# First experts' results combined inside the second self-attention, with a new order of its products

## The chip, the cores and the metric

The kernel runs on one core of a Trainium2 chip. The metric is the device time of one launch in microseconds. The engines are named PE or TensorE (matmul; PEld is its weight load), DVE or VectorE, ACT or ScalarE, POOL or GpSimd, and SP, which issues transfers.

## The reference

A decoder of two layers on 16 sequences (batches) of 256 tokens with 256 features, all float32. The part that the change touches:

```
# layer 0: the last step, a mixture of experts (8 experts, 2 for each token)
n  = layernorm(x)                      # (x - mean) / sqrt(var + 1e-5)
o  = w0(token) * E_i(n) + w1(token) * E_j(n)      # E(n) = gelu(n Wup) Wdown, the token's two best experts
x  = x + (n + layernorm(o))
# layer 1: self-attention, 16 heads of 64
n  = layernorm(x)
q, k, v = n Wq + bq, n Wk + bk, n Wv + bv
x  = x + softmax(q k^T / 8) v Wo + bo  # softmax over the keys, head by head
```

After it come layer 1's cross-attention and its mixture of 64 experts. Matmuls whose inputs are called high and low are float32 products split in three (high high, high low, low high).

## The kernel before, in words

x stays in SBUF as 32 tiles of 128 tokens (`sh.x`), two to a batch; `sh.stats` holds mean and variance of each token, `sh.rstd` the inverse root. The kernel is a row of blocks; within a block each engine runs its own program in order, and semaphores order them; a block ends for all engines together. `clear_semaphores` is a block of its own that resets the counters used so far.

The stretch around the change:

- `l0_experts_tiles` ends with the experts' rows written to a table in DRAM (`scratch.results`).
- `l0_experts_combine` (L3033) is a block for all 32 tiles in groups of four. POOL gathers two rows for each token (L3066); ACT scales the first (L3078); DVE adds the second, scaled (L3104), and takes the statistics of the sum (L3108, L3111); ACT takes the square root (L3084), DVE its reciprocal and an offset (L3117 to L3119); ACT scales x and adds the offset (L3091); DVE adds the normalised sum (L3126) and takes the statistics of the new x (L3131, L3134). In the same block the weights of the coming attention are loaded by SP (L1368), split into high (ACT, L1377) and low (DVE, L1382), and the bias of v is multiplied by Wo on TensorE (L1396).
- `clear_semaphores`, then `norm_scales` (L284), a block that makes `sh.rstd` of all 32 tiles with ACT's square root and DVE's reciprocal.
- `l1_attention` (L1406) goes over the batches, from -1 to 16. A batch has eight slots h, one for each pair of heads. In a slot TensorE makes the scores of pair h (L1499), turns the probabilities of pair h-3 (L1508), makes products called pieces, and multiplies the probabilities of pair h-4 with v (L1519). DVE takes the maximum of the scores (L1648), inverts the sums of pair h-1 (L1653), copies the turned probabilities (L1660), takes the low part of the output of pair h-5 (L1664) and the low parts of the pieces (L1670, L1674). ACT makes the exponents (L1574) and the high parts (L1598, L1584, L1587) or the copy of v (L1592). POOL multiplies the probabilities by the inverted sums (L1623) and adds the output bias to x once a batch (L1634).
- The pieces are in `order` (L1450): C is the key and query product of a pair, V a quarter of v, W half of the output product (L1684 adds it to x, and after the second half L1688 takes the new statistics), X the turning of half of the normalised x (L1531). Each names its number, how many batches it is ahead, and its slot. Pieces go to two PSUM banks in turn (`fill[i % 2]`), and a piece waits until the one before it in its bank is drained. The high and low parts of the output, `outT`, have one buffer for a batch; ACT therefore waits for W of the batch before, before it takes out the first pair (L1597).
- Scores have one PSUM buffer, so the scores of a pair wait for the exponents of the pair before it (L1494). The normalised x of the next batch (L1642) is made at the end of slot 2.
- The loop over the batches is rolled for batches 3 to 14 on every engine.

Of the kernel before, what the change touches and what calls it, by code (L numbers as in the profile page):

```python
# [14 lines left out]
P = 128  # L15
# [250 lines left out]


ROOT_GUESS = float(0x5f3759df)
ROOT_STEPS = 14


def inverse_root(engine, step, out, var, spare):


    step.then(engine.tensor_scalar(var, var, EPS, None, ALU.add))
    step.then(engine.tensor_scalar(out.bitcast(I32), var.bitcast(I32), -0.5, ROOT_GUESS, ALU.mult, ALU.add))
    for n in range(3):
        step.then(engine.tensor_tensor(spare, out, out, ALU.mult))
        step.then(engine.tensor_tensor(spare, spare, var, ALU.mult))
        step.then(engine.tensor_scalar(spare, spare, -0.5, 1.5, ALU.mult, ALU.add))  # L280
        step.then(engine.tensor_tensor(out, out, spare, ALU.mult))
# [1124 lines left out]
def l1_attention(nc, sh, prepared):  # L1406
# [11 lines left out]
    with ExitStack() as ctx:  # L1418
# [17 lines left out]
        outT = both("outT", [P, PAIRS, SEQ])  # L1436
        parts = sb("parts", [P, TPB, 6])
        means = sb("means", [P, TPB, 2])
# [5 lines left out]
        per_batch = {"X": KC, "C": PAIRS, "V": 4, "W": TPB}  # L1444
# [8 lines left out]
        assert len(order) % 2 == 0 and len(order) == sum(per_batch.values())  # L1453
# [5 lines left out]
        def prior_in_bank(i, b):  # L1459


            back = 0
            while True:
                i -= 2
                if i < 0:
                    i, back = i + len(order), back + 1
                if isinstance(b, int) and b - back < -1:
                    return None
                kind, number, ahead = order[i][0:3]
                if live(b - back + ahead):  # L1470
                    return kind, done(kind, number, b - back + ahead)

        def over_batches(engine, batch):


            for b in range(-1, 3):
                batch(b)
            with engine.Fori(3, BATCH - 1) as b:
                batch(b)
            batch(BATCH - 1)  # L1480
            batch(BATCH)

        def lagging(b, h, lag):

            own, pair = (b, h - lag) if h >= lag else (b - 1, PAIRS + h - lag)
            return (own, pair) if live(own) else None

        with nc.Block() as block:

            @block.tensor  # L1490
            def _(pe):
# [31 lines left out]
                def piece(i, kind, number, own, b):  # L1523
                    bank = fill[i % 2]
# [3 lines left out]
                    if kind == "X":  # L1528
                        pe.wait_ge(s_xn, own + 1)
                        for t in range(TPB):  # L1530
                            last = pe.transpose(bank[:, t * P:(t + 1) * P], xn[:, t, number * P:(number + 1) * P], sh.ident[:])  # L1531
# [11 lines left out]
                    elif kind == "W":  # L1543
                        t = number
                        pe.wait_ge(s_olow, PAIRS * (own + 1))
                        last = split_product(pe, bank[:, 0:DIM], [([a[:, c, t * P:(t + 1) * P] for a in outT],
# [3 lines left out]
                def batch(b):  # L1550
                    for h in range(PAIRS):
# [7 lines left out]
                        for i, kind, number, ahead in pieces:  # L1559
                            piece(i, kind, number, b + ahead, b)  # L1560
# [6 lines left out]
            def _(act):  # L1567
# [10 lines left out]
                def drain(i, kind, number, own):  # L1578
                    bank = fill[i % 2]
# [3 lines left out]
                    if kind == "X":  # L1583
                        act.copy(xT[0][:, number, :], bank[:, 0:SEQ]).then_inc(high["X"], 1)  # L1584
# [9 lines left out]
                def take_out(b, h):  # L1594
# [3 lines left out]
                    act.copy(outT[0][:, h, :], o_ps[h % 2][:, 0:SEQ]).then_inc(s_ohigh, 1)  # L1598

                def batch(b):  # L1600
                    for h in range(PAIRS):
                        taking = lagging(b, h, TAKE)
                        last_pair = taking and taking[1] == PAIRS - 1
                        if last_pair:
                            take_out(*taking)
                        if live(b):
                            exponents(b, h)
                        if taking and not last_pair:
                            take_out(*taking)
# [1864 lines left out]
```

## Time and profile before

| | us |
|---|---|
| median of 3 runs | 3141.59 (3135.95 to 3143.5) |
| the profiled execution | 3120.02 |
| its span | 3118.3 |
| mean granted TensorE clock | 0.907 of full speed |

| engine | busy us | share of the span |
|---|---|---|
| PE | 2555.6 | 82% |
| PEld | 2131.8 | 68% |
| DVE | 2057.3 | 66% |
| ACT | 1424.4 | 46% |
| POOL | 881.3 | 28% |

The shares are means over stages that differ: the combine takes some 100 us, the attention after it some 830 us. A number in brackets behind a row of the timeline is the idle time of that engine just before the instruction, and behind the arrow stands what ended it.

### The profile page before, as it was taken

Reading aid. Unit: us, or ns where it says so; the run is one execution under the profiler, and the core shown is the slowest. Engines: PE = TensorE matmul, PEld = TensorE weight load, DVE = VectorE, ACT = ScalarE, POOL = GpSimd, SP = SyncE. Lnnn points to the kernel's source line nnn. Section 1 sums busy time; section 2 is a strip of 40 time slices with the busy share of each in tenths; the row PEclk is TensorE's granted clock in tenths of the full one; section 3 lists DMA queues with packets and bytes.
Section 4 is the critical chain, followed back from the end, with each engine's and each line's share of the span. In section 5 each row is a group of like instructions: output and inputs, shape, how many; then the busy total and the mean of one; then the engine's idle time right before and its main releaser. Section 6 shows DMA issues by size and latency. Waiting matters only on the chain. (4 is left out here: it accounts for less than half of the span.)

```text
span 3118.3 us, 59168 instructions
## 1 busy us (share of the span) xinstructions
PE 2555.6 (82%) x19764; PEld 2131.8 (68%) x19764; DVE 2057.3 (66%) x4353; ACT 1424.4 (46%) x3350; POOL 881.3 (28%) x1026
## 2 busy tenths in 40 slices
PE   5978699999862999999149999999999679997483
PEld 4866588888752999999137777777777666665131
DVE  5863698989643777776566666666666547775664
ACT  1520334343330777776345554555454337665032
POOL 0000345454316000000633333333333103333266
PEclk8987799999975999999569999999999889999576
DMA  8000000000077765654400000000000463221745
GB/s 286 0 2 0 1 1 0 0 0 0 27 259 265 270 227 210 228 210 151 146 26 1 1 0 0 0 0 0 0 0 1 142 190 89 83 84 30 241 132 169
DMA packets 165273, 270.61 MB, mean 87 GB/s; under 512 B 21088, under 2 KB 140592, under 8 KB 151856
## 3 DMA queue, kind: packets, MB, share of 16 engines
q1 hardware_dynamic: 151008, 226.14, 21.5%
q0 software_dynamic: 9216, 25.18, 2.5%
q10 hardware_dynamic: 4944, 17.96, 1.5%
q8 instruction: 57, 0.93, 0.1%
q14 instruction: 48, 0.39, 0.0%
HBM read 191.85 MB, written 77.37 MB: 86 GB/s over the span
## 5 line engine op out<-in xcount | busy, mean ns | idle before, releaser
L1623 POOL TENSOR_TENSOR a_prob<-a_prob,a_rden 128x1024 f32<-128x1024 f32 x128 | 242.6, 1895 | 574.1 <-DVE a_rden L1653 574.1
L1574 ACT ACTIVATE a_prob<-a_s_ps,a_ntop 128x256 f32<-128x256 f32 x512 | 236.0, 473 | 353.8 <-DVE a_ntop L1648 353.8
L3066 POOL DMA_INDIRECT e0c_ya<-sorted_results,e_slots x64 | 67.9, 1061 | 507.8 <-POOLq L2869 488.6
L2306 DVE TENSOR_REDUCE x1a_top<-x1a_s_ps 128x4 f32<-128x1024 f32 x128 | 155.9, 1222 | 82.0 <-PE x1a_s_ps L2134 80.7
L2231 ACT ACTIVATE x1a_prob<-x1a_st_ps,x1a_mask_now 128x512 f32<-128x512 f32 x256 | 162.3, 686 | 91.5 <-PE x1a_st_ps L2150 90.1
L1648 DVE TENSOR_REDUCE a_ntop<-a_s_ps 128x4 f32<-128x1024 f32 x128 | 156.3, 1221 | 67.0 <-PE a_s_ps L1499 67.0
L1161 ACT ACTIVATE x0b_sq<-x0b_f 128x1024 f32<-128x1024 f32 x64 | 67.9, 1060 | 282.4 <-DVE x0b_f L1235 282.3
L68 PE MATMUL e0x_up_ps<-e0x_xT_high,e0x_up_w_high 128*128 128x256 f32 x624 | 180.4, 289 | 1.7 <-DVE e0x_up_w_low L2997 1.7
L68 PE MATMUL e0x_up_ps<-e0x_xT_high,e0x_up_w_low 128*128 128x256 f32 x624 | 177.6, 285 | 0.0
L68 PE MATMUL e0x_up_ps<-e0x_xT_low,e0x_up_w_high 128*128 128x256 f32 x624 | 177.4, 284 | 0.0
L68 PE MATMUL e0x_y_ps<-e0x_down_w_high,e0x_hT_high 128*128 128x256 f32 x624 | 176.6, 283 | 0.0
L68 PE MATMUL e0x_y_ps<-e0x_down_w_low,e0x_hT_high 128*128 128x256 f32 x624 | 176.6, 283 | 0.0
L68 PE MATMUL e0x_y_ps<-e0x_down_w_high,e0x_hT_low 128*128 128x256 f32 x624 | 176.6, 283 | 0.0
L1660 DVE COPY a_pT<-a_pT_ps 128x512 f32<-128x512 f32 x256 | 161.0, 670 | 0.7 <-PE a_pT_ps L1508 0.7
L1664 DVE TENSOR_TENSOR a_outT_low<-a_o_ps,a_outT_high 128x256 fp32r<-128x256 f32 x128 | 54.1, 423 | 149.0 <-ACT a_outT_high L1598 149.0
L1519 PE MATMUL a_o_ps<-a_pT,a_v 128*64 128x256 f32 x1024 | 141.4, 398 | 1.2 <-DVE a_outT_low L1664 1.2
L1508 PE MATMUL a_pT_ps<-ident,a_prob 128*128 128x128 f32 x1024 | 141.2, 281 | 0.0
L1674 DVE SCALAR_TENSOR_TENSOR a_kqT_low<-a_fill,a1w_kq_bias,a_kqT_high 128x256 fp32r<-128x256 f32 x256 | 109.3, 478 | 44.8 <-ACT a_kqT_high L1587 44.8
L3011 DVE TENSOR_TENSOR e0x_hT_low<-e0x_h,e0x_hT_high 128x512 fp32r<-128x512 f32 x156 | 104.4, 689 | 37.8 <-ACT e0x_hT_high L2977 37.8
L1508 PEld LDWEIGHTS a_pT_ps<-ident,a_prob 128*128 128x128 f32 x1024 | 110.5, 141 | 18.3 <-issue 1.6
L68 PEld LDWEIGHTS e0x_up_ps<-e0x_xT_high,e0x_up_w_high 128*128 128x128 f32 x624 | 120.7, 193 | 2.1 <-issue 2.1
L68 PEld LDWEIGHTS e0x_up_ps<-e0x_xT_low,e0x_up_w_high 128*128 128x128 f32 x624 | 120.6, 193 | 0.0
(579 smaller groups left out, 8520.2 us busy)
## 6 DMA issues: line engine op xcount, KB each, us to landing
e0x_up_raw<-up_rows SPq DMA_DIRECT2D x39, 1024.0 KB, 4.9
e0x_down_raw<-down_rows SPq DMA_DIRECT2D x39, 1024.0 KB, 5.6
x_qk<-head_rows SPq DMA_DIRECT2D x384, 64.0 KB
head_rows<-x1p_rows_out SPq DMA_DIRECT2D x32, 512.0 KB, 3.7
e1w_ew<-in_L_ffn_expert_w_dram SPq DMA_DIRECT2D x8, 2048.0 KB, 18.1
sorted_tokens<-zeros SPq DMA_DIRECT2D x10, 1024.0 KB, 12.4
e0x_xg<-sorted_tokens SPq DMA_DIRECT2D x39, 256.0 KB, 2.8
sorted_results<-e0x_y SPq DMA_DIRECT2D x39, 256.0 KB, 2.2
```

The lines of the kernel that those rows point to most:

```text
L68: last = pe.matmul(out, a[x], b[y], start=at == 0, stop=at == n - 1)
L1161: act.activation(sq[:, side % 2, :], f[:, p, side, :], ACT.Square).then_inc(s_sq, 1)
L1508: last = pe.transpose(pT_ps[n][:, j, t * P:(t + 1) * P], prob[:, h % RING, n, t, j * P:(j + 1) * P], sh.ident[:])
L1519: last = pe.matmul(o_ps[h % 2][DH * n:DH * (n + 1), 0:SEQ], v[:, j, at:at + DH], pT[:, h % 2, n, j, :], start=j == 0, stop=j == TPB - 1)
L1574: last = act.activation(prob[:, h % RING, n, t, :], s_ps[:, n, t * SEQ:(t + 1) * SEQ], ACT.Exp, bias=ntop[:, h % RING, n, t:t + 1], accum_ ...
L1623: last = pool.tensor_tensor(p, p, scale_of, ALU.mult)
L1648: dve.tensor_reduce(ntop[:, h % RING], s_ps[:].rearrange("p n (t s) -> p n t s", t=TPB), AXIS.X, ALU.max, negate=True).then_inc(s_top, 1)
L1660: dve.tensor_copy(pT[:, h % 2, n], pT_ps[n][:]).then_inc(s_pT, 1)
L1674: last = dve.scalar_tensor_tensor(kqT[1][:, number, side, :], bank[:, side * SEQ:(side + 1) * SEQ], kq_bias[:, side, number:number + 1], k ...
L2231: last = act.activation(prob[:, c % 2, j, 2 * (h % 2):2 * (h % 2) + 2, :], st_ps[:, :, j * SEQ:(j + 1) * SEQ], ACT.Exp, bias=mask_now[:, p ...
L2306: dve.tensor_reduce(dst, s_ps[h % 2][:].rearrange("p n (t s) -> p n t s", t=TPB), AXIS.X, ALU.max).then_inc(s_max, 1)
L3011: dve.tensor_tensor(part[1], h[:, n, :], part[0], ALU.subtract).then_inc(s_hl, 1)
```

## The change

- `clear_semaphores` goes ahead of the combine block; the one behind it and the `norm_scales` of the attention go.
- `l0_experts_combine` now combines batch 0 alone, beside the same loading and splitting of the weights. It gathers the rows of batches 0 and 1.
- The steps of the combine are methods of a class `Combine`, for one batch each. In batch b of the attention the combine of batch b+2 goes on: DVE mixes in slot 0, takes the statistics in slot 1; POOL makes the inverse root in slot 2; DVE makes the offset in slot 3; ACT scales x at the end of slot 3; DVE adds in slot 4 and takes the statistics of x in slot 5; POOL makes the second inverse root in slot 6. POOL gathers the rows of batch b+3 in slots 3 to 6, and ACT scales the first rows of batch b+3 at the end of slot 7. The normalisation of batch b+1 in slot 2 waits for its second root.
- The inverse roots are made by `inverse_root`, three Newton steps from an integer guess, 14 dependent small operations, and no longer by ACT's square root.
- `order` names the bank of each piece as its last number; x is turned in one piece of four transposes instead of two; the output product moves from slots 4 and 5 to 5 and 6; `outT` has two buffers.
- The rolled loop now holds two batches in each turn (batches 3 to 12) and POOL's program is not rolled.

```diff
-        order = [("C", 2, 0, 0), ("V", 0, 0, 0), ("C", 3, 0, 1), ("V", 1, 0, 1), ("C", 4, 0, 2), ("C", 5, 0, 3),
-                 ("C", 6, 0, 3), ("W", 0, -1, 4), ("C", 7, 0, 5), ("W", 1, -1, 5), ("V", 2, 0, 6), ("V", 3, 0, 6),
-                 ("X", 0, 1, 6), ("X", 1, 1, 6), ("C", 0, 1, 7), ("C", 1, 1, 7)]
+        order = [("C", 2, 0, 0, 0), ("V", 0, 0, 0, 1), ("C", 3, 0, 1, 0), ("V", 1, 0, 1, 1), ("C", 4, 0, 2, 0), ("C", 5, 0, 2, 1),
+                 ("C", 6, 0, 3, 0), ("C", 7, 0, 3, 1), ("V", 2, 0, 4, 0), ("V", 3, 0, 4, 1), ("W", 0, -1, 5, 0), ("X", 0, 1, 6, 0),
+                 ("W", 1, -1, 6, 1), ("C", 0, 1, 7, 0), ("C", 1, 1, 7, 1)]
...
-        outT = both("outT", [P, PAIRS, SEQ])
+        outT = both("outT", [P, 2, PAIRS, SEQ])
...
-                        wait_past(act, filled["W"], TPB * b)
+                        wait_past(act, filled["W"], TPB * (b - 1))
...
 # ACT, at the end of a slot
+                        if h == PAIRS - 1 and live(b + 3):
+                            combine.first(act, b + 3)
+                        if h == 3 and live(b + 2):
+                            combine.scale_x(act, b + 2)
...
 # POOL, in a slot
+                        if h == 2 and live(b + 2):
+                            combine.mix_root(pool, b + 2)
+                        if 3 <= h <= 6 and live(b + 3):
+                            combine.gather(pool, b + 3, h - 3)
+                        if h == 6 and live(b + 2):
+                            combine.x_root(pool, b + 2)
...
 # DVE, between the copies of the turned probabilities and the low part of the output
+                        if live(b + 2):
+                            if h == 0:
+                                combine.mix_rows(dve, b + 2)
+                            if h == 1:
+                                combine.mix_stats(dve, b + 2)
+                            if h == 3:
+                                combine.offset(dve, b + 2)
+                            if h == 4:
+                                combine.add(dve, b + 2)
+                            if h == 5:
+                                combine.x_stats(dve, b + 2)
...
+    def mix_rows(self, dve, c):
+        step.counted(dve.tensor_scalar(self.grow[:], sh.rstd[:, tiles], 1.0, None, ALU.add))
+        step.counted(dve.tensor_tensor(self.less[:], sh.stats[:, tiles, 0], sh.rstd[:, tiles], ALU.mult))
+        for t in range(TPB):
+            dve.wait_ge(self.s_first, TPB * c + t + 1)
+            dve.scalar_tensor_tensor(self.out[:, t, :], self.ya[:, t, 1, :], self.weights[:, 1, bass.ds(TPB * c + t, 1)],
+                                     self.out[:, t, :], ALU.mult, ALU.add).then_inc(self.s_mix, 1)
+    def offset(self, dve, c):
+        dve.wait_ge(self.s_r2, c + 1)
+        step.then(dve.tensor_tensor(self.shift[:], self.stat[:, :, 0], self.r2[:], ALU.mult))
+        dve.scalar_tensor_tensor(self.shift[:], self.shift[:], -1.0, self.less[:], ALU.mult, ALU.subtract).then_inc(self.s_shift, 1)
...
 # the block ahead of the attention, ACT and DVE
+                following.high(act, 0)
+                following.high(act, 1)
+                combine.first(act, 0)
+                following.high(act, 2)
+                combine.scale_x(act, 0)
+                following.high(act, 3)
+                combine.first(act, 1)
...
+                following.low(dve, 0)
+                following.low(dve, 1)
+                combine.mix(dve, 0)
+                combine.mix_root(dve, 0)
+                combine.offset(dve, 0)
+                following.low(dve, 2)
+                following.widen(dve)
+                combine.add(dve, 0)
+                combine.x_stats(dve, 0)
+                combine.x_root(dve, 0)
+                following.low(dve, 3)
+                following.bias_taken(dve)
```

## Rows read from the trace of the kernel before

**Rows 1.** busy time of each engine in two stretches; columns: stretch, us, busy us (instructions), TensorE clock, DMA share, GB/s.
```profile
1488.00:1595.00 107.00, 5.95 (x16) 4.58 (x16) 72.25 (x242) 41.13 (x78) 67.90 (x64) 0.53 0.40 122
...
2002.00:2053.00 51.00, 47.59 (x400) 38.93 (x400) 33.09 (x69) 26.27 (x94) 16.40 (x9) 1.00 0.00 0
```

**Rows 2.** timeline at the ends of the combine; columns: start us, us, engine, line, operation, tiles.
```profile
1489.79 0.18 DVE L3097 TENSOR_SCALAR e0c_grow<-x_rstd 128x32 f32<-128x32 f32 x1 [2.63 <-PEq L2869]
...
1590.39 1.40 DVE L3131 BATCH_NORM_STATS2 e0c_parts<-x_resident 128x6 f32<-128x256 f32 x4
...
1591.83 0.38 DVE L3134 BATCH_NORM_AGGREGATE x_stats<-e0c_parts 128x2 f32<-128x6 f32 x4
...
1593.56 0.18 DVE L298 TENSOR_SCALAR n_var<-x_stats 128x32 f32<-128x32 f32 x1 [1.35 <-PEq L108]
...
1595.00 0.74 DVE L1642 TENSOR_SCALAR a_xn<-x_resident,x_stats,x_rstd 128x256 f32<-128x256 f32 x2 [0.54 <-PEq L293]
...
1597.92 0.55 PE L68 MATMUL a_fill<-a_xT_high,a1w_wk_high 128*128 128x256 f32 x1 [1.01 <-DVE a_xT_low L1670]
```

**Rows 3.** DMA issues of 1487 to 1596: KB each, us from issue to landing.
```profile
a1p_w_nat<-in_L_attn_Wk_dram SPq DMA_DIRECT2D x1, 1024.0 KB, 8.5
```

**Rows 4.** timeline inside the combine, ACT and DVE.
```profile
1500.02 0.51 ACT L3078 ACTIVATE e0c_out<-e0c_ya,e_weights 128x256 f32<-128x256 f32 x1 [1.40 <-DMA e0c_ya<-sorted_results,e_slots]
...
1531.08 0.18 DVE L3117 RECIPROCAL e0c_r<-e0c_std 128x4 f32<-128x4 f32 x1
...
1531.29 0.16 DVE L3118 TENSOR_TENSOR e0c_shift<-e0c_stat,e0c_r 128x4 f32<-128x4 f32 x1
```

**Rows 5.** instructions by line, 1487 to 1596: busy us, mean ns, idle before.
```profile
L3104 DVE SCALAR_TENSOR_TENSOR e0c_out<-e0c_ya,e_weights,e0c_out 128x256 f32<-128x256 f32 x32 | 14.4, 482 | 26.1 <-ACT e0c_out L3078 26.1
...
L1382 DVE SCALAR_TENSOR_TENSOR a1w_wq_low<-a1p_w_nat,a1w_wq_high 128x2048 fp32r<-128x2048 f32 x1 | 2.3, 2282 | 0.0
```

**Rows 6.** TensorE's waits in the attention, 1600 to 2410: us in total, times, longest.
```profile
PE a_fill L1531 <- ACT a_v L1592: 29.0, 15, 2.1
...
PE a_fill L68 <- DVE a_outT_low L1664: 13.3, 15, 1.0
...
PE a_s_ps L1499 <- DVE a_kqT_low L1674: 5.3, 15, 0.4
```

**Rows 7.** timeline of DVE in one batch of the attention, 2002 to 2054.
```profile
2002.76 1.23 DVE L1648 TENSOR_REDUCE a_ntop<-a_s_ps 128x4 f32<-128x1024 f32 x1 [1.09 <-PE a_s_ps L1499]
...
2026.33 1.22 DVE L1648 TENSOR_REDUCE a_ntop<-a_s_ps 128x4 f32<-128x1024 f32 x1
...
2029.89 0.42 DVE L1664 TENSOR_TENSOR a_outT_low<-a_o_ps,a_outT_high 128x256 fp32r<-128x256 f32 x1 [1.09 <-ACT a_outT_high L1598]
...
2030.64 1.66 DVE L1674 SCALAR_TENSOR_TENSOR a_kqT_low<-a_fill,a1w_kq_bias,a_kqT_high 128x256 fp32r<-128x256 f32 x4 [0.32 <-ACT a_kqT_high L1587]
...
2032.54 1.21 DVE L1648 TENSOR_REDUCE a_ntop<-a_s_ps 128x4 f32<-128x1024 f32 x1
...
2053.72 1.23 DVE L1648 TENSOR_REDUCE a_ntop<-a_s_ps 128x4 f32<-128x1024 f32 x1 [1.09 <-PE a_s_ps L1499]
```

**Rows 8.** costliest groups of the page, the exponents.
```profile
L1574 ACT ACTIVATE a_prob<-a_s_ps,a_ntop 128x256 f32<-128x256 f32 x512 | 236.0, 473 | 353.8 <-DVE a_ntop L1648 353.8
```

**Rows 9.** timeline of POOL in the next stage, an inverse root.
```profile
2600.72 0.22 POOL L275 TENSOR_SCALAR x1a_gvar<-x1a_gvar 128x2 f32<-128x2 f32 x1
...
2604.95 1.24 POOL L2294 TENSOR_SCALAR x1a_gn<-x_resident,x_stats,x_rstd 128x256 f32<-128x256 f32 x1
```

**Rows 10.** timeline where POOL and DVE run together, and gathers.
```profile
699.71 1.90 POOL L1048 TENSOR_TENSOR x0b_f<-x0b_f,x0b_rnorm 128x1024 f32<-128x1024 f32 x1
...
699.77 2.92 DVE L1266 TENSOR_TENSOR x0b_g<-x0b_f,x0b_rnorm 128x1024 f32<-128x1024 f32 x1
...
1523.28 0.95 POOL L3066 DMA_INDIRECT e0c_ya<-sorted_results,e_slots  x1 [0.30 <-issue]
...
1525.78 2.64 POOL L3066 DMA_INDIRECT e0c_ya<-sorted_results,e_slots  x1 [0.31 <-issue]
```

More of the change, by code:

```diff
@@ L265 @@
 STATS_STEPS = 3
[L268 to L281, printed above, removed]
 def norm_scales(nc, sh, name, twice=False):
@@ L1476, in over_batches @@
             for b in range(-1, 3):
[L1477 to L1481, printed above, removed]
+                batch(b, b % 2)
+            with engine.Fori(1, (BATCH - 4) // 2) as pair:
+                for p in range(2):
+                    batch(2 * pair + (1 + p), 1 - p)
+            for b in range(BATCH - 3, BATCH + 1):
+                batch(b, b % 2)
         def lagging(b, h, lag):
@@ L1529, in piece @@
                         pe.wait_ge(s_xn, own + 1)
-                        for t in range(TPB):
-                            last = pe.transpose(bank[:, t * P:(t + 1) * P], xn[:, t, number * P:(number + 1) * P], sh.ident[:])
+                        for k in range(KC):
+                            for t in range(TPB):
+                                last = pe.transpose(bank[:, k * SEQ + t * P:k * SEQ + (t + 1) * P], xn[:, t, k * P:(k + 1) * P],
+                                                    sh.ident[:])
                     elif kind == "C":
@@ L1583, in drain @@
                     if kind == "X":
-                        act.copy(xT[0][:, number, :], bank[:, 0:SEQ]).then_inc(high["X"], 1)
+                        act.copy(xT[0][:].rearrange("p k s -> p (k s)"), bank[:]).then_inc(high["X"], 1)
                     elif kind == "C":
@@ L3030, in _ @@
                 over_groups(dve, step)
[L3033 to L3053 removed]
+ROOT_GUESS = float(0x5f3759df)
@@ new lines, in inverse_root @@
+def inverse_root(engine, step, out, var, spare):
+    step.then(engine.tensor_scalar(var, var, EPS, None, ALU.add))
+    step.then(engine.tensor_scalar(out.bitcast(I32), var.bitcast(I32), -0.5, ROOT_GUESS, ALU.mult, ALU.add))
+    for n in range(3):
+        step.then(engine.tensor_tensor(spare, out, out, ALU.mult))
+        step.then(engine.tensor_tensor(spare, spare, var, ALU.mult))
+        step.then(engine.tensor_scalar(spare, spare, -0.5, 1.5, ALU.mult, ALU.add))
+        step.then(engine.tensor_tensor(out, out, spare, ALU.mult))
@@ L3094, in _ @@
+                following.high(act, 1)
[4 more added lines that the diff above has]
+                combine.first(act, 1)
             @block.vector
             def _(dve):
-                step = Steps(dve, s_own)
-                dve.tensor_scalar(grow[:], sh.rstd[:], 1.0, None, ALU.add)
-                step.then(dve.tensor_tensor(less[:], sh.stats[:, :, 0], sh.rstd[:], ALU.mult))
@@ L3100, in mix @@
-                def mix(g):
-                    for t in range(g * G, (g + 1) * G):
-                        dve.wait_ge(s_first, t + 1)
-                        dve.scalar_tensor_tensor(out[:, g % OUTS, t % G, :], ya[:, t % GATHERS, 1, :], weights[:, 1, t:t + 1],
-                                                 out[:, g % OUTS, t % G, :], ALU.mult, ALU.add).then_inc(s_mix, 1)
-                    dve.wait_ge(s_mix, (g + 1) * G)
-                    for i in range(G):
-                        last = dve.bn_stats(parts[:, i, :], out[:, g % OUTS, i, :])
-                    step.then(last)
-                    for i in range(G):
-                        last = dve.bn_aggr(stat[:, g % 2, i, :], parts[:, i, :])
-                    step.then(last)
-                    dve.tensor_scalar(std[:, g % 2, :], stat[:, g % 2, :, 1], EPS, None, ALU.add).then_inc(s_var, 1)
```

239 lines of the change are left out of this document (132 added, 107 removed).

## The prediction

> **What bounds the kernel now.** I read the busy time by stretch first. The reader is to see two stretches in it [rows 1]: from 1488 to 1595 TensorE works 5.95 of 107 us and DVE, ACT and POOL share the work; in one batch in the middle of the attention (2002 to 2053) TensorE is busy 47.59 of 51 us at the full clock of 2.4 GHz, DVE 33.09, ACT 26.27, POOL 16.40. So the combine stage has no matmul that matters, and the attention is a TensorE stage whose other engines have room. Second, the timeline at the seams [rows 2]: the combine's DVE starts at 1489.79, its last statistics end at 1592.2, a block that clears semaphores and one for the square root follow, the attention starts at 1595.00 and the first key product at 1597.92. Third, TensorE's waits in the attention [rows 6]: 29.0 us before the transpose of x (15 waits, for the ACT copy of v), 13.3 us before the output product (15, for outT_low), 5.3 us before scores (15, for kqT_low). Fourth, the DVE rows of one batch [rows 7], which show how the slots of a batch (one for each pair of heads) are chained: maximum, exponents on ACT, drains, next maximum. The batch lasts 2053.72 - 2002.76 = 50.96 us.
>
> **1. The combine stage becomes the combine of batch 0 beside the weights.** Removed: 1595.00 - 1489.79 = 105.2 us [rows 2]. What stands in its place, on DVE, which is last in it:
> - The clearing block now stands ahead: 1593.56 - 1592.21 = 1.35 us, so the stage starts at 1491.15 [rows 2].
> - Wk lands 8.5 us after its issue [rows 3], which is in the stage's first half microsecond: 1500.1. Its high part on ACT takes as the others do about 1.9 us (1502.0), its low part on DVE 2.28 [rows 5]: 1504.3. Batch 0's rows are there by then: the second tile's ACT step began at 1500.02 [rows 4], 1501.4 with the clearing.
> - Mixing: two small operations and two of 0.48 [rows 5], 1.15 with their waits; statistics of two tiles 1.4 (four cost 1.40 + 0.38 [rows 2], and the two added settles and memsets take back what half the tiles save). 1506.9.
> - The root by Newton steps: 15 dependent small operations at 0.21 (1531.29 - 1531.08 [rows 4]): 3.1; offset 0.4: 1510.4.
> - Low part of Wv 2.28, widening of the bias about 1.8, add 0.95, statistics of x 1.4, second root 17 x 0.21 = 3.5, low part of Wo 2.28: 1522.7. The bias product (TensorE's 5.95 us of [rows 1]) lies under the last four. Taking it 0.4 and the block's end 0.5: **1523.7**.
> This saves 1595.0 - 1523.7 = **71.3 us**. Ends: small operations at POOL's 0.28 instead of 0.21 (+2.2) and weights 5 us later give 64; DVE never waiting for Wk gives 75.
>
> **2. The batch before the first pays for batch 1.** Its DVE order is now mix, statistics, wait for POOL's root, offset, wait for ACT's scaling, add, statistics, and only then the low part of xT, for which all key products wait. From the attention's start: normalise 0.74, mix 1.15, statistics 1.4, POOL's root 15 x 0.28 = 4.2 (2600.72 to 2604.95 for the same steps [rows 9]), offset 0.4, ACT 1.15, add 0.95, statistics 1.4, low part of xT 0.7: first key product after some 12.5 instead of 1597.92 - 1595.00 = 2.9 us. **+9.6 us**. Here nothing covers it. In batch 0 no pairs wait to be turned and there is no output product, so its first slots are set by the chain of maximum, exponents and drains and not by TensorE; some of the combine's DVE work and ACT's first scaling show: **+1.5**, between 0 and 5.
>
> **3. The new order of products.** TensorE's work in a batch stays: 50.96 less its waits of 2.09 + 0.94 + 0.37 = 47.6 us. With named banks x is turned into bank 0 after an output product that DVE drained a slot earlier, and no longer behind two v products, so the 29.0 us go. The output product moves from slot 4 to slot 5, one slot after outT_low of the last pair is made, so the 13.3 us go. **-42.3 us**. The second outT buffer removes an ACT wait (ACT held the first pair until the output product was through), which was covered; alone I cost it at nothing, but it lets the first product move later.
>
> **4. What the combine puts into each batch.** DVE: 1.15 (slot 0), 1.4 (1), 0.4 (3), 0.95 (4), 1.4 (5), together 5.3 us; ACT: four operations of 0.5, 2.1 us; POOL: two roots, 4.2 + 4.7, and four gathers of 0.95 + 0.30 [rows 10], 14 us. POOL then works 30 of 48 us. Its product of a pair (1.9 us) is wanted by TensorE two slots later, 11 us, so the 4.2 us of a root behind it are covered. DVE's steps stand between the pT copies and the low part of outT, where it now idles about a microsecond for ACT: in the slot that begins at 2026.33 the low part starts at 2029.89, +3.56, after 1.09 us of idle time, so the copies ended at +2.5 [rows 7]. So 1.0 us of each is free, and the rest has room in slots that TensorE sets (5.8 us against a chain of 5.2 in those with one key product). Where they hurt:
> - Slots 2 and 3 now both drain two key products. In slot 3 of before the drain ends 5.9 us after the maximum (2030.64 + 1.66 - 2026.33), the last pair's outT_low is squeezed in, and the next maximum comes at +6.21 [rows 7]. Slot 2 becomes such a slot and has xn (0.73) as well: 6.65; slot 3 gets ACT's scaling of x (1.1 us) ahead of the last pair's outT_high: 7.0. TensorE needs 5.8 in each, lets the maximum lag, and is held only where exponents end (3.3 us after the maximum began: 1.2 for itself, four of 0.47 [rows 8] and the handoffs) later than it arrives: my sum over the slots gives 0.55 us at the start of slot 5.
> - Slot 6 drains x and then the output product with statistics: the next maximum is 0.4 us later, and the 0.37 us wait for the first key product becomes 0.65.
> - Taken off: 0.25 us of transposes that wait in slot 4.
> That is 0.58 us a batch: **+8.7 us** for 15. The floor is 0 (TensorE set everything); the ceiling, if none of it were covered, is 5.3 + 2.1 = 7.4 us a batch, 111 us.
> POOL's root ends 8.75 us after slot 2's maximum, and DVE asks for it at 9.3: the offset does not wait, by half a microsecond.
>
> **A contention that the trace shows.** DVE's product with two inputs in SBUF took 2.92 us when it began inside POOL's multiplication, of which only 1.08 lie after that one's end (699.71 + 1.90); and a gather's issue took 2.64 us where DVE's low part of Wq, 2.28 us and also with two such inputs, ran, and 0.95 without [rows 5, 10]. The combine's mixing and adding (two SBUF inputs) begin 2.5 us after a maximum and POOL's product runs until about +3.25: 0.7 us of delay in slots 0 and 4, which have that room. The Trainium skill ("SBUF — State Buffer", Who interferes with whom) states that a DVE instruction with two SBUF inputs contends with a GpSimd instruction that reads SBUF, and that whoever starts second is fully blocked; on the first pair the trace agrees. The page infers that such a DVE instruction leaves descriptor generation alone; on the second the trace disagrees, and the measurement decides. By the page the gathers would cost nothing more, by the row up to 0.5 us each, in either case on POOL with 18 us to spare: the sum is the same unless this grows, which is rival A.
>
> **Sum**: -71.3 + 9.6 + 1.5 - 42.3 + 8.7 = **-93.8 us**. The profiled execution took 3120.0 us (span 3118.3), so its like would take 3026. The median of the runs shown is 3141.6, 0.7% above the profiled one; the time that I name goes by the median: 3141.6 - 94 = **3047.6 us**.
>
> **The rivals.**
> - A. The layout's gain is eaten: the drains of slots 2 and 3, the blocked DVE steps and the handoffs over POOL and ACT hold TensorE some 2.8 us a batch instead of 0.58 (the 42 us come back). For it: DVE goes from 33 to 38.5 us a batch, 79% of 48.5, with two slots over 6.6 us in a row. Against: they lag without holding TensorE in my sum. -60 us, 3082. Chance 0.2.
> - B. Everything is covered and the short stage is at its better end: -106, 3036. For it: slot 2 of before had 1.3 us of lag that TensorE never felt. Against: slot 3's ACT order is certain to be longer. 0.12.
> - C. The short stage is not short: the weights, their splits, roots and the bias product form one line on DVE and take 60 us instead of 32. Against: every term has a row. -66 and less, 3076. 0.05.
> - D. Slower. DVE's offset waits in slot 3 for POOL's root, with the drains of two key products and outT_low behind it, and TensorE behind them. The saving without this is 102.5 us; spread over 15 batches it is lost from 6.8 us of wait a batch, that is, from a root of 11.0 us instead of 4.2. For it: POOL's product, the bias addition and the root are one queue and the margin is only 0.5 us. Against: 0.28 us a step where POOL does it now [rows 9]. At 8 us a batch the time is +18, 3160. 0.04.
> - E. The forecast, within 3032 and 3066: 0.59.
> A change under 0.3%, 9 us, cannot be told from none. Cases E, B, A and C are faster: 0.95 with a little of D's approach to zero left to same (0.01); slower 0.04. The range takes in A and B and the bounds of points 1 and 4: 3025 to 3092.
>
> **What would show it.** Right: first attention instruction about 34 us after the combine block's first, first key product 12 us later; no wait of the x transpose for a_v, none of the output product for outT_low; a batch of 48.2 to 48.8 us between like maxima; POOL near 60% busy with POOL never named by TensorE. Wrong: waits of DVE's offset for r2, of ACT's first step for the gathers, or of scores for a_prob in every batch (A or D); a batch over 50 us (A); over 40 us between the first DVE instruction of the combine and the attention's start (C).

## The result and the profile after

| | median, us | runs | ratio to before, 95% |
|---|---|---|---|
| before | 3140.3 (3135.95 to 3143.5) | 4 | |
| after | 3017.03 (3011.59 to 3022.18) | 4 | 0.9608 [0.9586, 0.9630] |
| forecast | 3047.6 (range 3025 to 3092) | | 0.970 |

The change takes 123 us off, 29 more than forecast, and the time lies 8 us below the range. The profiled execution of after took 3018.96 us (span 3017.3), near its median; that of before had taken 3120.0, below its own. Stages that the change does not touch move between executions: the experts before the combine took 638.8 us in the profile of before and 649.1 in that of after, and the two profiled spans differ by 101.0 us only. So I compare stage by stage.

The page of after, its busy time by engine:

```profile
span 3017.3 us, 59401 instructions
PE 2543.4 (84%) x19764; PEld 2126.7 (70%) x19764; DVE 2098.6 (70%) x4492; ACT 1414.3 (47%) x3324; POOL 970.7 (32%) x1491
```

Busy time by stretch, the short stage and one batch, as in [rows 1] (stretch, us, then PE, PEld, DVE, ACT, POOL busy, clock, DMA share, GB/s):

```profile
1499.00:1534.00 35.00, 6.13 (x16) 4.69 (x16) 21.49 (x70) 10.33 (x10) 7.63 (x8) 0.60 0.51 162
1833.00:1880.00 47.00, 45.37 (x386) 37.53 (x386) 39.18 (x90) 27.66 (x97) 26.72 (x44) 1.00 0.04 13
```

The first row has what [rows 1] showed in 107 us; the second shows a batch in 47 us instead of 51, DVE 6 us and POOL 10 us busier in it. The timeline at the seams, as in [rows 2]: the experts' last copy, the low part of the weights that stands first in DVE's new stage, the attention's first instruction and the first key product:

```profile
1498.66 0.69 DVE L3036 COPY e0x_y<-e0x_y_ps 128x512 f32<-128x512 f32 x1 [5.06 <-PE e0x_y_ps L68]
...
1509.52 2.29 DVE L1366 SCALAR_TENSOR_TENSOR a1w_wq_low<-a1p_w_nat,a1w_wq_high 128x2048 fp32r<-128x2048 f32 x1 [10.17 <-ACT a1w_wq_high L1361]
...
1533.46 0.74 DVE L1646 TENSOR_SCALAR a_xn<-x_resident,x_stats,x_rstd 128x256 f32<-128x256 f32 x2 [0.54 <-PEq L3188]
...
1545.11 0.55 PE L68 MATMUL a_fill<-a_xT_high,a1w_wk_high 128*128 128x256 f32 x1 [9.74 <-DVE a_xT_low L1675]
```

From the experts' last copy to the attention's start it is 1533.46 - 1498.66 = 34.8 us; in before it was 1595.00 - 1486.47 = 108.5. The price is in the last row: the first key product starts 11.65 us into the attention and TensorE has waited 9.74 us for xT_low, where [rows 2] had 2.9 and 1.01. TensorE's waits in the attention (us in total, times, longest), as in [rows 6]:

```profile
PE a_s_ps L1490 <- DVE a_kqT_low L1679: 12.7, 15, 2.0
...
PE a_fill L68 <- DVE a_xT_low L1675: 9.7, 1, 9.7
PE a_s_ps L1490 <- ACT a_prob L1567: 8.4, 15, 1.4
```

The waits for v are gone, and those for outT_low ahead of the output product too but for one of 1.0 us; scores wait more, for kqT_low (5.3 us in [rows 6]) and for the exponents (5.1 in before).

Where the time went, from the profiles (attention: from its first DVE instruction to the first of the next norm, in before 1595.00 to 2429.32, in after 1533.46 to 2324.26):

| | forecast | measured |
|---|---|---|
| the stage between the experts and the attention | -71.3 | -73.7 |
| attention | -22.5 | 790.8 - 834.3 = -43.5 |
| all other stages | 0 | +16.2 |

### The profile page after: what moved, and what is told of

Its sections match the earlier page's. It is cut to its first block and busy times, and to the rows that moved or that the text cites. A ratio compares the mean times of both kernels' runs of the same rounds, so it can differ in the third digit from the quotient of the medians.

```text
span 3017.3 us, 59401 instructions
## 1 busy us (share of the span) xinstructions
PE 2543.4 (84%) x19764; PEld 2126.7 (70%) x19764; DVE 2098.6 (70%) x4492; ACT 1414.3 (47%) x3324; POOL 970.7 (32%) x1491
## 5 line engine op out<-in xcount | busy, mean ns | idle before, releaser
L1018 POOL TENSOR_TENSOR x0b_tree<-x0b_f 128x1024 f32<-128x1024 f32 x32 | 76.4, 2389 | 156.5 <-DVE x0b_f L1219 154.2
L2976 ACT CAST e0x_xT_high<-e0x_t_ps 128x512 fp32r<-128x512 f32 x39 | 22.9, 587 | 218.3 <-PE e0x_t_ps L2937 218.3
```

The lines of the kernel that those rows point to most:

```text
L1018: step.then(pool.tensor_tensor(tree[:], src[:, :, 0:HD // 2], src[:, :, HD // 2:HD], ALU.add))
```

## The experiments

### The layout alone, the combine alone, the second buffer alone

Three kernels that each do one part of the change. The layout alone takes over the order, the banks, the one piece in which x is turned and two output buffers, and leaves the combine its own stage. The combine alone keeps the order, the banks, x in two pieces and one output buffer (here and below the lines with a minus are those of the kernel after):

```diff
- order = [("C", 2, 0, 0, 0), ("V", 0, 0, 0, 1), ..., ("W", 0, -1, 5, 0), ("X", 0, 1, 6, 0), ("W", 1, -1, 6, 1), ...]
+ order = [("C", 2, 0, 0), ("V", 0, 0, 0), ..., ("W", 0, -1, 4), ("C", 7, 0, 5), ("W", 1, -1, 5), ("V", 2, 0, 6), ...]
- outT = both("outT", [P, 2, PAIRS, SEQ])
+ outT = both("outT", [P, 1, PAIRS, SEQ])
```

The third is the kernel before with `outT` of two sides, the take-out of pair 0 waiting for the output product of the batch before the last (`TPB * (b - 1)`). Because the side of the buffer goes by parity, its loop holds two batches in each turn, as in after, and POOL's program is not rolled; all three kernels have this in common.

> The new order of products with named banks and two output buffers, with the combine stage of before in front. Theory M (the gain of the layout was mis-sized: in the trace of after a steady batch has 46.6 us of TensorE work and 0.9 us of waits where before had 50.96 in all, so removing a wait also removes the slow restart around it): a batch of 46.9 to 47.2 us, the attention some 60 us shorter than before, the kernel 58 to 62 us faster (3078 to 3082). Rival F (the forecast's sizes, 42 us of removed waits and nothing else): 42 us faster, 3098, and the rest of the 123 us is in the stage in front.

> The combine inside the attention with the order, banks and single output buffer of before. Theory M: the short stage gives 73.7 us, the batch before the first takes back 8.8, and the combine's steps hold TensorE some 0.6 us a batch more, 9 us: 54 to 58 us faster, 3082 to 3086; with e1 the sum is near 118. Rival C (the waits of the old layout, 2.1 and 0.9 us a batch, cover the combine's stalls): 65 us faster, 3075. Rival O (overlap in the other sense: the old layout's lags and the combine's steps meet in the same slots): under 45 us faster.

> Before, with two buffers for the output alone; the loop over the batches holds two batches in each turn because the buffer goes by parity. The forecast costs this at nothing (within 0.3% of 3140): ACT's wait for the output product goes, TensorE's waits for a_v and for outT_low stay. Rival: slot 5, 8.96 us long before, shortens because the exponents behind the take-out come earlier: 0.5 us a batch, 7 us faster or more.

> The kernel before once more, for a second profiled execution. Its first profiled execution took 3120.0 us and its timed runs 3136 to 3144. Theory V (executions vary in the stages ahead of the combine): about 3140 us, with the 20 us in layer 0's cross-attention and experts, and the attention at 834 us. Rival A (the variation is in the attention): the attention takes some 850 us.

| | median, us (before 3128.3) | ratio, 95% | attention, us | a batch, us |
|---|---|---|---|---|
| layout alone | 3070.2 | 0.9821 [0.9805, 0.9837] | 780.8 | 47.1 to 48.9 |
| combine alone | 3103.9 | 0.9923 [0.9906, 0.9939] | 892.9 | 53 to 57 |
| two buffers alone | 3102.7 | 0.9921 [0.9904, 0.9937] | 811.1 | 48.9 to 50.7 |
| before once more | 3124.5 | | 835.2 | 51.0, a few 52 |

The profile of before repeats within 1 us in the attention, and its time lies with that of its neighbours and not at 3140. Then there are two surprises. First, the buffer that I had costed at nothing takes 25 us off by itself. TensorE's waits in the attention of that kernel:

```profile
PE a_fill L68 <- DVE a_outT_low L1666: 13.1, 15, 1.0
...
PE a_fill L1522 <- ACT a_v L1583: 5.2, 15, 0.8
```

Beside [rows 6] the wait for outT_low has stayed and the one for v fell from 29.0 to 5.2. So what held the transpose of x was mostly not the order of banks: ACT, which copies v, stood in slot 5 at the take-out of pair 0, waiting for both output products to leave the only buffer, and its copies of v came late. ACT's take-out of pair 0 and its copy of v in one batch of before, where the maximum of slot 5 begins at 2293.92:

```profile
2299.22 0.37 ACT L1598 CAST a_outT_high<-a_o_ps 128x256 fp32r<-128x256 f32 x1 [2.02 <-PE a_fill L68]
...
2306.28 1.10 ACT L1592 COPY a_v<-a_fill 128x512 f32<-128x512 f32 x2
```

and the same two with the second buffer alone, where it begins at 2275.00:

```profile
2278.07 0.39 ACT L1589 CAST a_outT_high<-a_o_ps 128x256 fp32r<-128x256 f32 x1
...
2285.55 1.10 ACT L1583 COPY a_v<-a_fill 128x512 f32<-128x512 f32 x2
```

The take-out comes 3.1 us after the maximum instead of 5.3, the copy of v 10.6 instead of 12.4, and slot 5 takes 7.22 us instead of 8.96, as the rival of this run had it. The row of waits names the last releaser (v), not what had held the releaser. The gain is not the changed loop's: rolled batches go from 50.96 to 49.23 us, written-out ones from 50.54 (batch 2) to 48.89, and the loop over two batches has more of the stops that are shown further down.

Second, the combine in its old surroundings costs the attention 50 to 59 of the 74 us that its short stage gives (108.5 to 34.7 us there): -24 us in all. In its waits both of [rows 6] are there, the one for outT_low more than doubled:

```profile
PE a_fill L68 <- DVE a_outT_low L1666: 30.3, 15, 2.3
PE a_fill L1522 <- ACT a_v L1583: 29.2, 15, 2.2
```

Of the theories, M came near for the layout (58 to 62 us expected) and failed for the combine, where rival O (under 45 us) held. The parts (-56 and -24) do not add to -123: more than 40 us are in their meeting. (The profiled execution of the combine alone took 3114.4 us, 10 above its median; its attention of 892.9 may be high by some of that.)

### Where the parts meet

Two more kernels split this. One is the combine with the old order and banks but two output buffers. The other is the kernel after with the first half of the output product back in slot 4, behind the transposes that it waits for; the last two v products move to slot 5 for it, with other banks:

```diff
- ("V", 2, 0, 4, 0), ("V", 3, 0, 4, 1), ("W", 0, -1, 5, 0), ("X", 0, 1, 6, 0),
+ ("W", 0, -1, 4, 0), ("V", 2, 0, 5, 1), ("V", 3, 0, 5, 0), ("X", 0, 1, 6, 0),
```

> The combine in the batches with the old order of products and the old banks, but two output buffers. Combine alone took 24 us off and cost the attention some 4 us a batch (50.96 to about 55); two buffers alone brought a batch to 49.2. Theory 1, what made the combine dear was the single output buffer (the combine delays the waiting transposes, and each delay was passed on through W1): a batch of 49.2 to 50, a time of 3140 minus 73 minus 15 to 25, so 3040 to 3052, ratio 0.968 to 0.972. Theory 2, it was the old place of the products (W0 right behind the transposes, the new batch's X behind them): the batch stays at 53 or more, 3085 to 3105, ratio 0.982 to 0.989.

> The kernel after, with only the first half of the output product W0 put back in slot 4 behind the transposes it waits for, and the second pair of V in slot 5. Theory 1, W0's later slot is what hides the waiting transposes and the combine: a wait of TensorE for outT_low of about 2 us a batch comes back in slot 4, 15 batches x 2 = 30 us, so about 3045 to 3050, ratio 0.970. Theory 2, the two buffers and the earlier X do it: within 6 us of the kernel after, ratio 0.960 to 0.963.

The first: 3065.3 us, ratio 0.9808 [0.9793, 0.9823] (before 3125.4). It falls between the two theories, close to the second: batches of 49.4 to 53.8 us, TensorE still waiting 30.6 us for outT_low ahead of the output product (15 times) and 4.8 for v. With it the price of the combine in the attention can be read in each surrounding, without the gain of its stage:

| the attention has | without the combine | with it | price | price by the ratios |
|---|---|---|---|---|
| one output buffer, old order | 834.3 | 892.9 | 58.6 | 50 |
| two output buffers, old order | 811.1 | 843.6 | 32.5 | 38 |
| two buffers, new order | 780.8 | 790.8 | 10.0 | 7 |

The last column is the difference of the two timed ratios times 3128 us, plus the stage's 73.7; for the first, (0.9923 - 1) x 3128 + 73.7 = 50. The profiles give 26 us of the fall to the second buffer and 22 to the new order, the ratios 12 and 31; both say that each has a part (each step of the last column is uncertain by some 7 us). Of the 10.0 us left, 8.3 are in the batch before the first (18.8 us from its start to the first maximum, 10.5 with the layout alone) and 1.5 in batch 0 (42.4 for 40.9), which leaves about nothing for the others.

The traces say where the price lies in the old order, and it is not at the output product alone. DVE's offset in slot 3 of a batch of this first kernel, ACT's scaling of x behind it, and the first output product of slot 4:

```profile
2224.66 1.84 DVE L3146 TENSOR_TENSOR e0c_shift<-e0c_stat,e0c_r 128x2 f32<-128x2 f32 x1 [0.79 <-POOL e0c_r L3141]
2226.73 0.60 ACT L3153 ACTIVATE x_resident<-x_resident,e0c_shift,e0c_grow 128x256 f32<-128x256 f32 x1 [0.41 <-DVE e0c_shift L3147]
...
2229.07 0.38 PE L68 MATMUL a_fill<-a1w_wo_high,a_outT_high 128*128 128x256 f32 x1 [2.26 <-DVE a_outT_low L1666]
```

DVE waits for POOL's root in all 14 batches, 0.78 us each (0.76 in the combine alone), ACT waits for DVE, the last pair's take-out stands behind ACT's scaling, and TensorE waits for its low part: slot 3 takes 7.4 us instead of 6.1 and slot 4 up to 6.8 instead of 5.3. That is the chain of rival D, and it ran in both kernels of the old order. The old order has one key product in slot 2, which takes 5.7 us there and 6.5 in the new one, so DVE asks for the root 0.8 us sooner. How much of the 33 to 59 us is this late root, and how much the place of the output product, no run tells: the old order with the root a slot earlier was not tried.

The second: 3025.5 us, ratio 0.9684 [0.9669, 0.9699], nearer to the first theory. A wait of this kind comes back, at half the size that I gave it:

```profile
PE a_fill L68 <- DVE a_outT_low L1668: 13.2, 15, 1.2
```

Slot 4 goes from 4.42 to 5.25 us and a batch from 47.6 to 48.3; the attention takes 801.2 instead of 790.8 us. The ratio says more, +0.0076 or 24 us with some 8 of uncertainty. With the combine and two buffers, order and banks together give 843.6 - 790.8 = 52.8 us by the profiles (63 by the ratios); W's slot is 10.4 (24) of them, a fifth to two fifths, and not all. The rest was not taken apart into order, banks and the one piece of x: the transpose of x ahead of the last v products overwrites xT while these still read it, and the new order with one output buffer has the take-out of pair 0 waiting for a product behind the scores that it must release. Neither was tried.

### How much room POOL has

The prediction gave POOL's root a margin of 0.5 us and a price only from a root of 11.0 us. Two kernels: the root one slot earlier, and 15 more small POOL operations ahead of its last step, which double it (+4.2 us):

```diff
- if h == 2 and live(b + 2):
+ if h == 1 and live(b + 2):
      combine.mix_root(pool, b + 2)
```

```diff
+ for n in range(15):
+     idle.then(engine.tensor_scalar(self.idle[:], self.var[:], 1.0, None, ALU.mult))
```

> After, with POOL's first inverse root in slot 1 instead of slot 2. In the trace of after the offset of slot 3 took 1.84 us instead of 0.16, because POOL's product of a pair, pushed behind the root, ran at the same time. Theory P (the two-input DVE step and POOL's product exclude each other): with the root a slot earlier the product of slot 3 runs 0.5 us earlier, the offset takes about 0.9 us, the gap between the maxima of slots 3 and 4 falls from 6.62 to 6.3 or less; as TensorE has slack there, the batch shortens by at most 0.3 us, 0 to 5 us in all. Rival: the mixing statistics are ready too late for slot 1, POOL's product of slot 2 is late and the batch is 0.5 us or more longer.

> After, with 15 more dependent small operations in POOL's first inverse root of each batch (4.2 us; their result is not used). This is rival D of the prediction at a price of 4.2 us. Rival D (DVE's offset waits for the root and TensorE behind it): root ready 3.9 us after DVE asks for it, of which TensorE's slack in slots 3 and 4 takes 0.5: 3 to 3.5 us a batch, 45 to 52 us slower than after, 3065. Rival S (the lag of DVE is made up in the slots with one drain): under 1 us a batch, less than 15 us slower.

Earlier: 3015.9 us, ratio 0.9604 [0.9586, 0.9621], no difference from after that can be measured (before 3139.8; attention 787.5). The offset fell to 0.90 us as expected, but slot 3 only from 6.60 to 6.53, not to 6.3. Doubled: 3105.7, 0.9890 [0.9871, 0.9909]: 88 us slower than after for 4.2 us a batch, above what both theories said. A batch takes 53.4 to 53.7 us. The rows of the slot in question, the end of POOL's root in after and DVE's offset there:

```profile
2142.59 0.22 POOL L3144 TENSOR_SCALAR e0c_r<-e0c_r 128x2 f32<-128x2 f32 x1
2142.77 1.90 POOL L1620 TENSOR_TENSOR a_prob<-a_prob,a_rden 128x1024 f32<-128x1024 f32 x1
...
2142.85 1.84 DVE L3149 TENSOR_TENSOR e0c_shift<-e0c_stat,e0c_r 128x2 f32<-128x2 f32 x1
2144.72 0.16 DVE L3150 SCALAR_TENSOR_TENSOR e0c_shift<-e0c_shift,e0c_less 128x2 f32<-128x2 f32 x1
```

and the same DVE line, with the root doubled:

```profile
2003.51 1.84 DVE L3154 TENSOR_TENSOR e0c_shift<-e0c_stat,e0c_r 128x2 f32<-128x2 f32 x1 [4.36 <-POOL e0c_r L3149]
```

The root ends at 2142.81 and DVE starts the offset at 2142.85: there is no margin. It is 0.03 to 0.04 us in nine of the 14 batches and 0.3 in five. DVE does not wait, but it is held for the rest of POOL's product (below), and with the root doubled 4.36 us of wait stand ahead of that, with outT_low and kqT_low queued behind it, and TensorE waits 57.0 us (15 times, up to 4.7) for kqT_low ahead of a product, where after had 0.8: slot 3 goes from 6.6 to 10.8 us and slot 4 from 4.4 to 6.2. Rival D's mechanism is real, and DVE starts to wait with a root hardly longer than this one; the kernel was spared that by 0.04 us. Where between 4.2 and 8.4 us of root the time begins to rise was not run; an offset of 1.84 us instead of 0.90 cost slot 3 only 0.07.

### What is left: the loop, the first batch, and the offset

In the rolled loop of after five of the ten batches are 0.6 to 1.6 us longer at one place. After, at such a place, and the kernel with all batches written out, at the like place:

```profile
1784.04 0.39 PE L1490 MATMUL a_s_ps<-a_kqT_high 64*128 64x256 f32 x2 [1.78 <-DVE a_kqT_low L1679]
```

```profile
1778.47 0.39 PE L1485 MATMUL a_s_ps<-a_kqT_high 64*128 64x256 f32 x2 [0.36 <-DVE a_kqT_low L1674]
```

Three kernels: all batches written out (`for b in range(-1, BATCH + 1)` in place of the loop); the batch before the first with the low part of xT ahead of the combine of batch 1; and these two together with the earlier root. A fourth adds to the third that ACT makes the offset:

```diff
- step.then(dve.tensor_tensor(self.shift[:], self.stat[:, :, 0], self.r2[:], ALU.mult))
- dve.scalar_tensor_tensor(self.shift[:], self.shift[:], -1.0, self.less[:], ALU.mult, ALU.subtract)
+ for t in range(TPB):
+     act.activation(self.shift[:, t:t + 1], self.stat[:, t, 0:1], ACT.Identity, scale=self.less_r2[:, t:t + 1],
+                    bias=self.less[:, t:t + 1])
```

> After, with the batches of the attention written out on every engine and no rolled loop. In the trace of after the rolled batches (3 to 12) take 47.5 us and every second one 1.1 to 1.6 us more at slot 7 or 0, and the batches written out 47.0. Theory L (rolling costs it: addresses from registers and the jump back on all engines): 5 jumps x 1.3 us + 10 x 0.5 us = 11 us faster than after, 3006 if after is 3017 (0.3 to 0.4%). Rival I (longer programs cost more instruction loading than the jumps): no faster than after.

> After, with the combine of batch 1 moved behind the low part of xT of batch 0 in DVE's order (mixing and statistics behind it, offset behind the two key products, add and statistics of x in the first slot of batch 0; ACT and POOL accordingly). Forecast's step 2 (the DVE order in the batch before the first costs 9.6 us, measured 8.8): the first key product comes 3 us after the attention's start instead of 12.5, some 2 to 3 us come back in slot 0 of batch 0: 6 to 7 us faster than after, 3010. Rival (the first maxima wait for the combine of batch 1 all the same): under 2 us faster.

> The kernel after with all batches of the second attention written out (alone about -15 us against after), the first batch's order changed so that its key products come before the waiting combine (alone -7 to -9) and the root a slot earlier (alone nothing). Theory 1, the gains lie in different places and add: -22 to -24 against after, ratio 0.953, about 2994. Theory 2, part of the first batch's gain is given back since batch 0 grew: ratio 0.955 to 0.956, about 3001.

> As the kernel with the three together, with the combine's offset made by ScalarE from POOL's root instead of by VectorE, so that VectorE no longer waits for POOL nor has a step that POOL's product holds up (1.84 us where 0.16 is the step alone). Theory 1, VectorE's held-up step is what makes slot 3 6.6 us: slot 3 falls to 6.2, 0.3 us a batch, -5 us, ratio 0.951 to 0.952. Theory 2, TensorE's work fills the batch (46.5 of 47.0 us): no difference, ratio within 0.001 of the three together.

| | median, us | ratio, 95% | attention, us |
|---|---|---|---|
| after | 3017.0 | 0.9608 [0.9586, 0.9630] | 790.8 |
| written out | 3002.3 | 0.9561 [0.9540, 0.9582] | 777.5 |
| first batch reordered | 3010.5 | 0.9577 [0.9558, 0.9596] | 785.8 |
| three together | 2989.6 | 0.9566 [0.9552, 0.9579] | 773.1 |
| and the offset on ACT | 3000.2 | 0.9599 [0.9586, 0.9612] | 785.6 |

(Before took 3139.8 beside the second and third, 3125.4 beside the last two; the ratios are to be compared, not the times.) Written out, every batch takes 47.0 us: 11.2 of the 13 us are in the ten batches of the loop, as theory L had it, and 2 in the batch before the first and batch 0, which the loop does not hold and which differ by a microsecond each between kernels of the same order anyway. Reordered, the first maximum comes 10.3 us into the attention instead of 18.8, but batch 0 takes 45.6 us instead of 42.4, so 5.0 of 8.5 us stay. Together they make the attention 17.7 us shorter, about the sum of the two; the ratio gives -0.0042, 13 us, below the 22 expected, with an uncertainty of 8 us that takes in 18. By its attention this is the best version that was run; by the ratios it cannot be told from the written-out one.

The offset on ACT is a miss that says most about the order. It frees DVE of the held step (0.90 us there) and yet costs 10 to 13 us: slot 3 goes from 6.53 to 7.22 us, and little else moves. ACT and DVE in slot 3, first three together, then with the offset on ACT:

```profile
1695.40 1.14 ACT L3169 ACTIVATE x_resident<-x_resident,e0c_shift,e0c_grow 128x256 f32<-128x256 f32 x2
1696.39 0.42 ACT L1590 CAST a_outT_high<-a_o_ps 128x256 fp32r<-128x256 f32 x1
...
1696.84 0.42 DVE L1673 TENSOR_TENSOR a_outT_low<-a_o_ps,a_outT_high 128x256 fp32r<-128x256 f32 x1 [0.31 <-ACT a_outT_high L1590]
1697.18 1.22 DVE L1657 TENSOR_REDUCE a_ntop<-a_s_ps 128x4 f32<-128x1024 f32 x1
```

```profile
1695.60 0.71 ACT L3166 ACTIVATE e0c_shift<-e0c_stat,e0c_less,e0c_less_r 128x1 f32<-128x1 f32 x2
1696.34 1.09 ACT L3174 ACTIVATE x_resident<-x_resident,e0c_shift,e0c_grow 128x256 f32<-128x256 f32 x2
1697.34 0.35 ACT L1590 CAST a_outT_high<-a_o_ps 128x256 fp32r<-128x256 f32 x1
...
1697.72 0.42 DVE L1673 TENSOR_TENSOR a_outT_low<-a_o_ps,a_outT_high 128x256 fp32r<-128x256 f32 x1 [1.00 <-ACT a_outT_high L1590]
1698.06 1.21 DVE L1657 TENSOR_REDUCE a_ntop<-a_s_ps 128x4 f32<-128x1024 f32 x1
```

The two new ACT operations take 0.71 us, and the last pair's copy, DVE's low part of it and the next maximum all come that much later: 0.69 in the slot. ACT, with 28 of 47 us busy, is what sets slot 3, because ACT's scaling of x stands ahead of the last pair's take-out. Both theories had looked at DVE or TensorE only.

## Why the prediction was wrong, by its steps

**Step 1, right.** The stage gave 73.7 us for 71.3 forecast. DVE waited 10.17 us for the high part of Wq and 1.42 more for that of Wk, whose low part ended 16.9 us after the experts' last copy began (17.8 by the forecast's 1504.3), and the root ran on DVE at 0.2 us a step (1517.77 to 1520.73), as forecast.

**Step 2, right for the combine, with a term of the layout left out.** The batch before the first cost 8.7 us against before for 9.6 (by the first maximum 7.6 in the written-out kernel). Batch 0 was to cost 1.5 more and took 2.8 less (42.4 us for 45.2), but the layout alone has it at 40.9: the combine costs it 1.5 us (0.5 in the written-out kernel), and what I had left out is that the new order and the second buffer shorten this batch by 4.3.

**Step 3, the failed step.** "The second outT buffer removes an ACT wait ..., which was covered; alone I cost it at nothing": alone it is worth 25 us. The 42.3 us that the waits of [rows 6] hold did go, but the 29.0 of them were put down to the place of the transpose and the banks, and belonged mostly to the one buffer. The sum of the layout was mis-sized as well: 834.3 - 780.8 = 53.5 us for 42.3. "TensorE's work in a batch stays" is the term: the 47.6 us between its waits became 46.55 in after. A steady batch fell by 50.96 - 47.56 = 3.40 us, which is 3.03 of named waits and 1.02 of such work, less 0.65 of longer waits for kqT_low and the exponents. I had taken all that lies between named waits for work that stays. What the microsecond was is open: the trace has the same 396 matmuls in a batch and counts TensorE busy for 47.7 us in before and with the second buffer alone, 47.0 with the layout alone and 46.7 in after, so it went with the order and lay in time that the profile calls busy. The sum also had nothing for the loop over two batches, which the change brings along; it costs 11 us against written-out batches, where the loop of before cost some 8 by its one written-out batch without a stop, so the term is small.

**Step 4, the second mis-sized term.** The combine was to cost 0.58 us a batch, 8.7 us. All of its price in the attention, with the two terms of step 2, is 10.0 us by the profiles, 7 by the ratios, and by the split above about 0.2 us is left for the 15 batches. Slot 3 was forecast at 7.0 and slot 2 at 6.65. In the written-out batches of both kernels slot 2 is 6.45 with and without the combine, slot 3 goes from 6.12 to 6.60, through ACT as I said, and slot 4 gives it back, from 4.82 to 4.34: the maximum lags TensorE in slot 3, and TensorE is never held long enough for it to count. What I did not see is that this depends on the order: the same combine costs 33 to 59 us in the old one. The contention came where it was forecast, in slots 0 and 4: the combine's first step there takes 0.91 us and its first addition 1.2 instead of 0.5. The gathers did not meet it: all 64 took 0.9 to 1.0 us. The margin of 0.5 us for POOL's root was nil (its end came 8.9 us after slot 2's maximum for 8.75, and DVE asked at 9.0 and not at 9.3), and the offset's 1.84 us in place of 0.16 did little harm (slot 3 is 6.53 us in the written-out batches with the root a slot earlier and 6.61 in after's), because DVE would have waited a microsecond for ACT's copy there anyway.

**The rivals.** A is refuted by the batch of 47 to 47.6 us, C by the stage of 34.8. B ("everything is covered", 3036) was nearest and still too small, since it too took TensorE's 47.6 us for a floor. D did not happen in this kernel; its chain ran in the two kernels of the old order, and the doubled root shows a price of 6.0 us a batch for 4.2 us of root.

**What was missed in sum.** Of the 29.5 us, 11.2 are the layout's, 9.8 the combine's (19.8 forecast in the attention, 10.0 measured) and 2.4 the stage's, together 23.4. The other 6 are within what the untouched stages differ between the profiled executions.

## What to carry to other kernels

A wait names its last releaser only: before a gain is written on it, ask what held that releaser's engine, and treat a single buffer that an in-order engine waits on as a wait of everything behind it on that engine. A floor made of "span less named waits" is not a floor: another order went under it by 2% with the same matmuls. Work put beside a tight stage is cheap only where its engines' queues have slack at that very place, so change the order first and then put the work in. Work ahead of the copy that the next maximum hangs on cost the slot its whole length (0.69 of 0.71 us), whatever the engine's mean load; putting it behind that copy is the next thing to try and was not run.

## What the runs showed of the hardware

- Small DVE operations are held by a POOL product as well. A scaling of 128x2 elements, 0.16 us by itself, took 0.91 us in after, ending with POOL's product, and the offset above 1.84:

```profile
2123.78 1.90 POOL L1620 TENSOR_TENSOR a_prob<-a_prob,a_rden 128x1024 f32<-128x1024 f32 x1 [3.27 <-DVE a_rden L1657]
```

```profile
2124.80 0.91 DVE L3117 TENSOR_SCALAR e0c_grow<-x_rstd 128x2 f32 x1
2125.62 0.15 DVE L3118 TENSOR_TENSOR e0c_less<-x_stats,x_rstd 128x2 f32 x1
```

  The product ends at 2125.68 and the held step at 2125.71. The two copies of pT out of PSUM that DVE made inside the same product (2123.62, 1.26 us) took their usual time. So the price of the hold goes by what is left of POOL's product and not by the size of DVE's step; the prediction's example, 2.92 us, was a large step [rows 10].
- The loop over two batches cost 11 us of attention over what the written-out batches take: a stop of 0.6 to 1.6 us in five of its ten batches, in slot 7 or 0, and 0.56 us a batch besides (47.56 against 47.0). The loop over one batch of before costs 0.42 us a batch (50.96 against 50.54 in batch 2), with a stop of 1.3 us in two of its twelve; before has one as long in batch 1, which is written out. What a stop is made of, no run shows.
- The issue of a gather took 2.3 to 2.6 us the four times that it began beside a DVE instruction of 2.28 us with two inputs in SBUF, for 0.95 in 51 of the 64 of before.
